# Routing cut into pieces among the first shared-expert chunks, one more token group ahead of the experts, and scatter rows written by ScalarE

## The reference, cut to what matters

```python
scores = softmax(xt @ gate_w.T)                    # 4096 tokens, 8 experts
_, idx = top_k(scores + gate_bias, 2)
weights = take_along_axis(scores, idx, axis=1)
for e in range(8):
    gate_e = sum(where(idx == e, weights, 0), axis=1)
    h = silu(xt @ w1[e].T) * (xt @ w3[e].T)
    y = y + gate_e[:, None] * (h @ w2[e].T)
z = silu(xt @ sw1.T) * (xt @ sw3.T) @ sw2.T        # the shared experts, 512 wide
return y + z                                       # then the residual x + (y + z)
```

## Time and profile before

| | us |
|---|---|
| median of 3 runs | 684.58 (682.52 to 685.39) |
| profiled execution, its own time | 679.88 |
| span of its profile | 678.1 |
| PE busy in the span | 573.9 (85%) |
| DVE busy | 449.8 (66%) |
| ACT busy | 339.8 (50%) |
| POOL busy | 211.7 (31%) |

### The profile page before, as it was taken

The page is one execution under the profiler, slowest core; times in us unless marked ns, Lnnn a source line. Parts: engine busy times, 40 slices in busy tenths (PEclk is TensorE's granted clock), DMA queues, the critical chain, the costliest instruction groups (busy, mean ns, idle before and its releaser), DMA issues.

```text
span 678.1 us, 11259 instructions
## 1 busy us (share of the span) xinstructions
PE 573.9 (85%) x3484; PEld 501.0 (74%) x3484; DVE 449.8 (66%) x1143; ACT 339.8 (50%) x710; POOL 211.7 (31%) x404
## 2 busy tenths in 40 slices
PE   3738989977498998684299899899999999998995
PEld 2727789977477998453278777688888888887884
DVE  4983898978578974878777776344444444444985
ACT  0416977614388781461454554255555555553331
POOL 2061120012323000000566777155455455452000
PEclk9978579979675999697599999899999999999998
DMA  9988000000000000920122222233333333325941
GB/s 283 313 246 3 1 1 1 2 0 1 1 0 1 2 1 1 347 118 1 55 79 87 91 91 86 79 102 102 109 105 102 106 103 106 104 79 177 383 161 62
DMA packets 57127, 62.59 MB, mean 92 GB/s; under 512 B 14736, under 2 KB 50448, under 8 KB 57072
## 3 DMA queue, kind: packets, MB, share of 16 engines
q1 hardware_dynamic: 49216, 43.46, 22.7%
q0 software_dynamic: 6480, 17.77, 7.3%
q10 hardware_dynamic: 1376, 0.66, 0.4%
HBM read 30.50 MB, written 31.37 MB: 91 GB/s over the span
## 4 chain that ended last, share of the span: by engine, by line
PE 42%; DVE 11%; ACT 4%; issue 3%; POOL 0%; DVEq 0%; ACTq 0%; POOLq 0%
PE bank L1208 12%; PE bank L1209 11%; PE bank L1210 11%; PE bank L1329 2%; PE bank L1345 2%; PE bank L1217 1%; DVE hf L1138 1%; ACT W_hi L911 1%; ACT h_hi L891 1%; DVE XN L974 1%; DVE XR L974 1%; DVE X L1129 1%; DVE XT_lo L1019 1%; DVE W_lo L1153 1%; DVE sw_lo L1027 1%
## 5 line engine op out<-in xcount | busy, mean ns | idle before, releaser
L843 POOL DMA_INDIRECT token_out<-YS,to_row x71 | 69.6, 980 | 96.1 <-ACT YS L941 92.5
L827 POOL DMA_INDIRECT slots_in<-XR,slot x64 | 69.8, 1091 | 82.5 <-DVE XR L1108 67.2
L575 PE MATMUL a_bank<-VO,E_hi 128*128 128x258 f32 x272 | 78.7, 289 | 4.3 <-DVE E_lo L482 4.3
L579 PE MATMUL a_bank<-VO,E_lo 128*128 128x258 f32 x272 | 78.1, 287 | 0.0
L577 PE MATMUL a_bank<-VO,E_hi 128*128 128x256 f32 x272 | 78.1, 287 | 0.0
L1179 DVE TENSOR_TENSOR hr<-bank,sr 128x256 f32<-128x256 f32 x71 | 30.1, 424 | 61.9 <-ACT sr L929 61.9
L453 DVE TENSOR_SCALAR E<-a_bank 128x512 f32<-128x512 f32 (+3 forms) x80 | 45.9, 606 | 29.3 <-PE a_bank L565 29.3
L1208 PE MATMUL bank<-W_hi,XST_hi 128*128 x142 | 62.4, 440 | 0.5 <-DVE XST_lo L1183 0.5
L1208 PE MATMUL bank<-XT_hi,sw_hi 128*128 128x512 f32 x128 | 52.4, 410 | 10.0 <-DVE XT_lo L1019 8.4
L929 ACT ACTIVATE sr<-bank 128x256 f32<-128x256 f32 x71 | 27.4, 385 | 64.1 <-PE bank L1210 64.1
L1210 PE MATMUL bank<-W_hi,XST_lo 128*128 x142 | 56.8, 400 | 0.0
(11 more groups left out here) (227 smaller groups left out, 1650.5 us busy)
## 6 DMA issues: line engine op xcount, KB each, us to landing
XS<-slots_in SPq DMA_DIRECT2D x71, 129.0 KB, 2.0
YG<-token_out SPq DMA_DIRECT2D x16, 512.0 KB, 7.8
slots_in<-blank SPq DMA_DIRECT2D x7, 1161.0 KB, 14.7
W_raw<-in_wT_dram SPq DMA_DIRECT2D x8, 768.0 KB, 12.6
X<-in_x_dram SPq DMA_DIRECT2D x8, 512.0 KB, 7.2
out_dram<-X SPq DMA_DIRECT2D x32, 128.0 KB, 2.1
token_out<-YS,to_row POOLq DMA_INDIRECT x71, 2.4
slots_in<-blank SPq DMA_DIRECT2D x1, 1032.0 KB, 13.7
```

The costliest lines, as they stand in the source:

```text
L575: pe.matmul(O_ps[Q % 2][j][:, 0:D + 2], E_hi[:, n % NE, cols], VO[:, kt, 0:D + 2], start=(kt == 0), stop=False)
L579: mm = pe.matmul(O_ps[Q % 2][j][:, 0:D + 2], E_lo[:, n % NE, cols], VO[:, kt, 0:D + 2], start=False, stop=(kt == qt))
L827: pool.indirect_dma_start(out=xs, out_offset=bass.IndirectOffsetOnAxis(ap=slot[k][:, t:t + 1], axis=0), in_=XR[:, t % 4, k, :], in_offset= ...
L843: pool.indirect_dma_start(out=ys, out_offset=bass.IndirectOffsetOnAxis(ap=to_row[:, i:i + 1], axis=0), in_=YS[:, i % NYS, :], in_offset=No ...
```

## The change

- The routing on VectorE is cut into functions (`probabilities`, `choice`, `both_choices`, `counts`, `slots`; the operations in them are the old ones) and called behind hf of chunks 0, 1, 2, 4 and 5; the weights of the choices and `slot_experts` follow in chunk 5. The counting matmuls move to chunk 4 and write into bank 0, which the transposes use too, so the third group's transposes wait for the counts.
- `HALF` is 6: six groups run ahead of the experts, two behind. Groups 5 and 6 of the routed results are both added in the last chunk.
- The scatter starts in chunk 5 with four tiles and goes on with 8/5 tiles a chunk until chunk 23.
- VectorE no longer writes the rows of XR. ScalarE writes both of each tile, behind `h_hi`: a copy from XN for the first eight tiles, and an Identity activation of X with scale `rstd` and bias `shifts` (a new 128 x 32 operation on VectorE) for the others.
- XN of the third group is made at the head of chunk 6 instead of in chunk 5. XN of groups 2 and 3, and the X adds of groups 2 to 5, wait until the rows are written that read what they overwrite.

```diff
-        TL_ps, L_ps, LT_ps, C_ps = (bank[0:2], bank[2:4]), bank[4:6], bank[6:8], bank[6:8]
+        TL_ps, L_ps, LT_ps, C_ps = (bank[0:2], bank[2:4]), bank[4:6], bank[6:8], (bank[0][:, 0:NT * NX], bank[0][:, NT * NX:2 * NT * NX])
-        HALF = 5
+        HALF = 6
+        COUNT_AT, SLOTS_AT = 4, 5
+        N_SLOTS = N_CHOSEN + 11
         def tiles_to_scatter(n):
-            return range(min(2 + 5 * n // 3, NT), min(2 + 5 * (n + 1) // 3, NT))
+            k = n - SLOTS_AT
+            return [] if k < 0 else range(GT) if k == 0 else range(GT + 8 * (k - 1) // 5, min(GT + 8 * k // 5, NT))
         def group_to_add(n):
-            return {2: [0], 3: [1], 4: [2], 5: [3], 6: [4], 7: [5], 9: [6]}.get(n - MC * HALF, [])
+            return {2: [0], 3: [1], 4: [2], 5: [3], 6: [4], 7: [5, 6]}.get(n - MC * HALF, [])
...
         @block.gpsimd
                 for k in range(TOPK):
-                    if k == 0:
-                        pool.wait_ge(s_xr, 2 * t + 2)
-                    else:
-                        pool.wait_ge(s_xr1, t + 1)
+                    pool.wait_ge(s_xr1, 2 * t + k + 1)
                     pool.indirect_dma_start(out=xs,
...
         @block.scalar
-            def second_row(t):
-                act.wait_ge(s_xr, 2 * t + 1)
-                if t >= 4:
-                    act.wait_ge(s_sc[t % 4], 16 * TOPK * (t // 4))
-                act.activation(XR[:, t % 4, 1, 0:D], XR[:, t % 4, 0, 0:D], ACT.Copy).then_inc(s_xr1, 1)
+            def scatter_rows(t):
+                act.wait_ge(s_xr, t + 1)
+                for k in range(TOPK):
+                    row = XR[:, t % 4, k, 0:D]
+                    if t < 2 * GT:
+                        act.activation(row, XN[:, t // GT, t % GT, :], ACT.Copy).then_inc(s_xr1, 1)
+                    else:
+                        act.activation(row, X[:, t, :], ACT.Identity, bias=shifts[:, t:t + 1],
+                                       scale=rstd[:, t:t + 1]).then_inc(s_xr1, 1)
             def shared(groups):
                 for G in groups:
                     for n in range(MC * G, MC * G + MC):
                         gate_silu(n)
+                        chunk_hi(n)
                         if G < HALF:
                             for t in tiles_to_scatter(n):
-                                second_row(t)
-                        chunk_hi(n)
+                                scatter_rows(t)
                         if n % MC == 2 and G + 1 in groups:
                             group_hi(G + 1)
                         if n < KC * NX:
...
-            second_row(0)
-            second_row(1)
+            act.wait_ge(s_shifts, 1)
             shared(range(HALF))
...
         @block.vector
+            dve.scalar_tensor_tensor(out=shifts[:, :], in0=mv[:, :, 0], scalar=-1.0, in1=rstd[:, :], op0=ALU.mult,
+                                     op1=ALU.mult).then_inc(s_shifts, 1)
...
             def group_xn(G):
+                if G in (2, 3):
+                    dve.wait_ge(s_xr1, TOPK * GT * (G - 1))
...
             def scatter_tile(t):
                 if t >= 4:
                     dve.wait_ge(s_sc[t % 4], 16 * TOPK * (t // 4))
-                normalised(XR[:, t % 4, 0, 0:D], t).then_inc(s_xr, 1)
                 dve.tensor_copy(XR[:, t % 4, :, D:RW], meta[:, t, :, :]).then_inc(s_xr, 1)
...
             def add_shared(G, z):
...
+                if 2 <= G < HALF:
+                    dve.wait_ge(s_xr1, TOPK * GT * (G + 1))
...
             def shared(groups):
                 for G in groups:
                     for n in range(MC * G, MC * G + MC):
+                        if n == SLOTS_AT + 1:
+                            group_xn(2)
                         dve.wait_ge(s_sg, n + 1)
...
                         if n == 0:
+                            probabilities()
+                        if n == 1:
+                            choice(0)
+                        if n == 2:
+                            choice(1)
+                            both_choices()
+                        if n == COUNT_AT:
+                            counts()
+                        if n == SLOTS_AT:
+                            slots()
+                            choice_weights()
                             slot_experts()
...
-                        if n % MC == 1 and G + 1 in groups:
+                        if n % MC == 1 and n != SLOTS_AT and G + 1 in groups:
                             group_xn(G + 1)
...
-            choice_weights()
-            scatter_tile(0)
-            scatter_tile(1)
             shared(range(HALF))
...
         @block.tensor
             def group_transpose(G):
                 pe.wait_ge(s_xn, N_XN + GT * G + GT)
+                if G == 2:
+                    pe.wait_ge(s_r, N_SLOTS)
...
                         if n > MC * groups[0]:
                             outputs(n - 1)
+                        if n == COUNT_AT:
+                            count_tokens()
...
-            pe.wait_ge(s_r, N_CHOSEN)
-            rhs = chosen[:, :, :].rearrange("p t e -> p (t e)")
-            pe.matmul(C_ps[0][:, 0:NT * NX], before[:, :], rhs, start=True, stop=True)
-            pe.matmul(C_ps[1][:, 0:NT * NX], ones_b[:, :], rhs, start=True, stop=True).then_inc(s_cnt, 1)
+            def count_tokens():
+                pe.wait_ge(s_r, N_CHOSEN)
+                pe.wait_ge(s_xtl, N_XTL + KC * 2)
+                rhs = chosen[:, :, :].rearrange("p t e -> p (t e)")
+                pe.matmul(C_ps[0], before[:, :], rhs, start=True, stop=True)
+                pe.matmul(C_ps[1], ones_b[:, :], rhs, start=True, stop=True).then_inc(s_cnt, 1)
```

More of the change, by code:

```diff
@@ L601, in attention_and_experts @@
         rstd = sb("rstd2", [P, NT])
+        shifts = sb("shifts", [P, NT])
         gate_raw = sb("gate_raw", [P, KC, NX])
@@ L1063, in _ @@
                                                   in1=biased[:, :, :], op0=ALU.mult, op1=ALU.add))
-            done(dve.tensor_tensor(chosen[:, :, :], pick[0][:, :, :], pick[1][:, :, :], ALU.add))
-            assert step[0] == N_CHOSEN
-            dve.wait_ge(s_cnt, 1)
-            done(dve.tensor_copy(total[:, :, :], C_ps[1][:, 0:NT * NX].rearrange("p (t e) -> p e t", t=NT)))
-            flat3 = [ap[:, :, :].rearrange("p e t -> p (e t)") for ap in (keep, total, upto)]
-            done(dve.tensor_tensor_scan(out=flat3[2], data0=flat3[0], data1=flat3[1], initial=0.0,
-                                        op0=ALU.mult, op1=ALU.add))
@@ L1073, in _ @@
-            done(dve.tensor_scalar(n_i[:, :], upto[:, :, NT - 1], float(P - 1), None, ALU.add))
-            done(dve.tensor_scalar(n_j[:, :], n_i[:, :], P.bit_length() - 1, None, ALU.logical_shift_right))
-            done(dve.tensor_copy(n_f[:, :], n_j[:, :]))
-            done(dve.tensor_tensor_scan(out=ends[:, :], data0=one8[:, :], data1=n_f[:, :], initial=0.0,
-                                        op0=ALU.mult, op1=ALU.add))
-            done(dve.tensor_tensor(base[:, :], ends[:, :], n_f[:, :], ALU.subtract))
@@ L1085, in _, with both_choices, counts @@
-            for k in range(TOPK):
-                done(dve.tensor_tensor(tmp[:, :, :], pick[k][:, :, :], slot_e[:, :, :], ALU.mult))
-                done(dve.tensor_reduce(red[:, :], tmp[:, :, :], AX.X, ALU.add))
-                done(dve.tensor_copy(slot[k][:, :], red[:, :]))
-            dve.sem_inc(s_slot, 1)
+            def both_choices():
+                done(dve.tensor_tensor(chosen[:, :, :], pick[0][:, :, :], pick[1][:, :, :], ALU.add))
+                assert step[0] == N_CHOSEN
+            def counts():
+                dve.wait_ge(s_cnt, 1)
+                done(dve.tensor_copy(total[:, :, :], C_ps[1].rearrange("p (t e) -> p e t", t=NT)))
+                flat3 = [ap[:, :, :].rearrange("p e t -> p (e t)") for ap in (keep, total, upto)]
+                done(dve.tensor_tensor_scan(out=flat3[2], data0=flat3[0], data1=flat3[1], initial=0.0,
+                                            op0=ALU.mult, op1=ALU.add))
+                done(dve.tensor_scalar(n_i[:, :], upto[:, :, NT - 1], float(P - 1), None, ALU.add))
+                done(dve.tensor_scalar(n_j[:, :], n_i[:, :], P.bit_length() - 1, None, ALU.logical_shift_right))
+                done(dve.tensor_copy(n_f[:, :], n_j[:, :]))
+                done(dve.tensor_tensor_scan(out=ends[:, :], data0=one8[:, :], data1=n_f[:, :], initial=0.0,
+                                            op0=ALU.mult, op1=ALU.add))
+                done(dve.tensor_tensor(base[:, :], ends[:, :], n_f[:, :], ALU.subtract))
+                done(dve.tensor_scalar(base[:, :], base[:, :], float(P), None, ALU.mult))
+                done(dve.tensor_tensor(upto[:, :, :], upto[:, :, :], total[:, :, :], ALU.subtract))
+                done(dve.tensor_tensor(upto[:, :, :], upto[:, :, :],
+                                       base[:, :].unsqueeze(2).to_broadcast([P, NX, NT]), ALU.add))
+                done(dve.tensor_tensor(slot_e[:, :, :], C_ps[0].rearrange("p (t e) -> p t e", t=NT),
```

(8 more changed lines are left out.)

20 lines of the change are left out of this document (8 added, 12 removed).

## The result

| | before | after |
|---|---|---|
| median of the runs, us | 684.99 (682.52 to 685.44, 4 runs) | 695.95 (695.28 to 697.72, 4 runs) |
| profiled execution, its own time | 679.88 | 695.28 |
| span of its profile | 678.1 | 693.5 |

The ratio is 1.0175, with a 95% interval of 1.0146 to 1.0204: slower by 11.0 us. The forecast was 694.5, slower.

What follows compares the result with a forecast made beforehand. No engine was full: VectorE's order set 5.0 us a chunk, and TensorE waited 16.14 us for the routing. Five terms sum to +9.9 us: 689.8 on the profiled 679.88, 694.5 on the median; range 682 to 702.

Steps and rivals of the forecast that it cites:

- 1. routing out of the hole, at hf(0): Ahead of chunk 0: routing leaves TensorE's hole, so VectorE's first operation there, hf(0), comes at 314.6, -15.4 us.
- 2. chunks 0 to 5: VectorE's operations add up in order, with the routing pieces inside: 40.6 us against 32.07, +8.5 us.
- 3. chunks 6 to 15: ScalarE's rows stand ahead of W_hi and VectorE's W_lo waits for it: 57.3 us against 50.24, +7.1 us.
- 4. chunks 16 to 23, way into the experts: TensorE paces to hf(23), then last scatters and slot loads hold the experts: 40.0 us against 17.74, +22.3 us.
- 5. two groups behind the experts: After the experts: four chunks and a transpose set go (-17.8), last-chunk adds and lower clock cost +4.0 and +1.2: -12.6 us.
- Faster: Chunks run at TensorE's pace, the wait before W_lo staying near 4 us in all: 679.9 us; chance 0.12.
- No change: Rows at 0.36 us (-4.4) and scatters done before TensorE is ready (-5.1), both needed: 685.0 us; chance 0.18.
- The clock: Chunks 6 to 15: TensorE's waits lower its granted clock, some 2 us more at three places: 700.5 us; chance 0.14.
- The table switch: Chunks 9 to 23: Identity and Silu in different ScalarE tables, two loads a chunk, +38 us: 733 us; chance 0.03.

Runs made afterwards that it cites:

- first experiment: The changed kernel with ScalarE's scatter rows moved from ahead of W_hi (and XT_hi) to behind it: 694.88 us, 1.0174 to the kernel before.

## Why the prediction was right, and where not

By its own steps, as differences of the two traced executions (predicted, then measured):

| step | predicted | measured |
|---|---|---|
| 1. routing out of the hole, at hf(0) | -15.4 | -15.2 |
| 2. chunks 0 to 5 | +8.5 | +7.7 |
| 3. chunks 6 to 15 | +7.1 | +10.7 |
| 4. chunks 16 to 23, way into the experts | +22.3 | +26.8 |
| 5. two groups behind the experts | -12.6 | -12.8 |
| head, experts | 0 | -1.8 |
| sum | +9.9 | +15.4 |

**Steps 1, 2 and 5 hold** within 0.8 us.

**Step 3 holds wherever no standstill lies.** The rows cost what was said (0.588 us against the bound of 0.60, following each other at 0.49 where the sum had 0.54), and W_lo waited for W_hi as said. The table of chunk lengths (first experiment) shows the sum chunk by chunk: for chunks 9 to 15 it gives 42.1 us, measured 41.3, none of them off by more than 0.35. The miss is in chunks 7 and 8, +1.6 and +2.9 us, where hf waited 1.8 and silu 4.5 us for a late signal. The step that failed is the silent one that nothing outside the lists holds TensorE's products up. No run has the change's own order without scatters; the first experiment's order takes 45.9 us without them and 57.4 with them. Against the second trace of before the step is +5.7: that trace has a standstill in the stretch (3.1 us ahead of XT_hi), and the first trace of before happened not to have one.

**Step 4 failed in one term:** "TensorE paces". hf(16) to hf(23) took 35.1 us in place of 29.3, with two standstills of 3.5 and 6.3 us in it; the three kernels without these scatters take 28.8 to 28.9. The way from hf(23) to the last scatter's end (5.6, predicted 6.9) and from there to the transposes (3.9, predicted 3.8) hold.

**Why the total came out all the same.** Steps 3 and 4 fell short by 8.1 us together, but a median run of before lies 5.1 us above its first trace and one of after only 0.7 above its own. The medians differ by 11.0, the forecast said 9.9. That the two come so close is luck: what the sum lacks in the kernel after was nearly made up by the distance of before's first trace from its median run.

**The right sum hid a wrong division.** The prediction booked the routing as a gain of 6.9 us at hf(6) and the sixth group as the loss. Done alone, the pieces cost 2.3% (1.5 to 3.0), the sixth group 0.7%; and on top of pieces and ScalarE's rows the sixth group gives 0.9% back (1.0263 to 1.0175). The scatters' times go with this. "Waits" is the time in which GpSimd waits for a row between them; the heads of the executions differ, so the start of the routing's exp stands beside them.

| kernel | routing's exp | first scatter | last one's end | between | of it waits | experts |
|---|---|---|---|---|---|---|
| before | 310.38 | 328.19 | 424.79 | 96.6 | 8.4 | 430.06 |
| before, second trace | 306.72 | 324.54 | 426.08 | 101.5 | 13.9 | 431.33 |
| six groups alone | 311.37 | 329.19 | 429.30 | 100.1 | 13.1 | 452.52 |
| pieces alone | 304.16 | 343.94 | 439.13 | 95.2 | 9.5 | 442.81 |
| after, five groups | 308.01 | 348.06 | 446.20 | 98.1 | 17.7 | 449.78 |
| after | 307.87 | 347.90 | 453.69 | 105.8 | 24.7 | 457.57 |
| after, rows on VectorE | 311.80 | 351.59 | 450.67 | 99.1 | 14.1 | 454.39 |

64 scatters took 95 to 106 us beside the chunks in all of these (111.9 in the one trace of the slots a chunk earlier), 80 to 88 of it GpSimd's own, the rest waits for rows. The routing in one piece delayed the chunks, but the first scatter came 17.8 us behind the routing's exp; in pieces it comes 39.8 to 40.1 behind it, 22 us later in every version, since the slots are known only behind five chunks. With the pieces alone GpSimd's waits are 9.5 us, too few to make up for 22, and TensorE stands 4.07 us ahead of the experts for the slots. How much of the loss is this later start and how much the standstills is not separated; the experiment made for it (slots one chunk earlier) is inconclusive. In the kernel before the X add comes last, and with six groups alone TensorE's chunks do (hf(23) at 447.18). In the kernel after GpSimd waits 24.7 us for rows, so there the chunks with their standstills hold the scatters up.

**The rivals.** Faster: its deciding point, the wait before W_lo, was 19.3 us; and with the wait gone the pace did not come either. No change: it needed scatters done before TensorE is ready, and they came last. The clock: its mechanism came, at three places in chunks 6 to 15 as it said. Behind waits of TensorE of 2.7, 2.3 and 2.5 us the granted clock is 0.50 or 0.51 in 368.6 to 372.0, 378.9 to 382.3 and 395.9 to 399.3 us, the level of 1.2 GHz; in the first trace of before it is 1.00 from 340 to 432. Its price of some 2 us each is not seen where the latter two lie: chunk 10 is 0.2 us shorter than the sum, chunk 13 0.3 longer; in chunk 8 it can't be told from the standstill. Ahead of the experts and in their first 6.6 us the clock is 0.50 again, and the 71 slots took 0.7 us longer. The table switch: none. The Trainium skill's statement (ScalarE: Activation LUTs, Table sets) that identity is in every set is borne out: in this stage there is one load of 1283 ns, ahead of the first silu.

Of the versions that compute the whole result none beats the kernel before by more than its interval.

## What to carry to other kernels

Before a hole on the busiest engine is filled by spreading out the work behind it, ask which serial chain starts at the end of that work; here it was 64 scatters, which started 22 us later behind the routing's start, and the 15 us of the hole did not come back. If taking a wait away doesn't move the total, don't yet conclude that the wait cost nothing: compare stage by stage, since the gain can be lost at another place, as it was here. And take a second trace of the kernel that a sum is made against, since one execution can lack a delay that the median run has.

## What was not expected of the hardware

GpSimd's indirect scatters beside the shared experts' chunks cost the other engines 19.3 us in 17 chunks: ScalarE and VectorE stand still for 2 to 8 us at a time for products that the records show as done, and TensorE's signals for them arrive late and bunched (443.64 and 443.92 us for products recorded until 437.34 and 441.47). The same bytes by SyncE's queue cost nothing that can be seen (74.80 us in both stretches), and the 71 scatters in the experts' stage bring no standstill.

The traces with standstills also lack records of signals. Of 33 each for seven of the stage's signals, the first trace of before, the one without scatters, the one with SyncE's writes and the one with a busy GpSimd have all 33, after has 26 to 31 and the second trace of before 27 to 31. The Trainium skill (NOTIFIC — the notification-queue block, Overflow: three behaviours, one of which stalls the engine) names three things that can happen when the ring for records is full: in one of them the record is dropped, in another the engine is held until there is room. No run here shows which is at work. Whether the recording causes the standstills is open: every run has a span and a clock from its records, so none shows the kernel without them.
